# A graph network kernel: edge scores, segment softmax and weighted sums as one stage with an online softmax, on one core

## The chip, the core and the metric

The kernel runs on one core of a Trainium2 chip. The metric is the device time of one execution in microseconds (us); the time before is the median of three runs. Matmuls run on TensorE (PE), elementwise work on VectorE (DVE) and ScalarE (ACT), gathers are issued by GpSimd (POOL), the other transfers by SyncE (SP) and ScalarE. SBUF is the on-chip memory, PSUM takes what TensorE computes.

## What is computed

A graph of 12,500 nodes with 256 features and 200,000 edges, sorted by destination, goes through two blocks. The first is graph attention with 8 heads of 32 columns, the second two graph convolutions and a dense layer. The first block is what the change rewrites:

```python
h = (relu(layernorm(x)) @ W.T).reshape(n, H, D)
h_src, h_dst = h[src], h[dst]
alpha = einsum('ehd,hd->eh', h_src, a_src) + einsum('ehd,hd->eh', h_dst, a_dst)
enc = relu(edge_attr @ edge_W.T + edge_b).reshape(-1, H, D)
alpha = alpha + sum(enc * h_dst, axis=-1)
alpha = where(alpha >= 0, alpha, 0.2 * alpha)
amax = segment_max(alpha, dst, n)
ex = exp(alpha - amax[dst])
attn = ex / maximum(segment_sum(ex, dst, n)[dst], 1e-10)
out = segment_sum(h_src * attn[..., None], dst, n).reshape(n, H * D) + bias
```

## The kernel before

Nodes lie in 98 tiles of 128. The program is a row of stages (functions ending in `_phase`), each closed by a barrier of all engines. Edges are cut into chunks of 128; a chunk that straddles two node tiles is worked through once for each, which makes 1664 steps, 16 steps to an iteration, 104 iterations.

`steps_phase` loads the edges, finds the tile and the rows of each step, and writes the lists to HBM. `node_phase` (through `dense_phase`) normalizes each tile of nodes and multiplies it by W; the result stays in SBUF (`h_all`) for the destination side and goes to HBM (`gat_table`) for the source side. `score_phase` computes a score for each edge and head. For a pair of chunks TensorE encodes the edge attributes (L870, bf16, in three parts that together hold a float32) and spreads the destination rows to the edges by a one-hot matmul in float32 (L875). ScalarE applies the relu (L772), VectorE multiplies (L817), sums over the 32 columns of each head (L820), and makes the one-hots (L807). GpSimd gathers the source rows, 128 at a time (L757), for their source scores; the gathered rows are stored to HBM (`gathered`). `softmax_phase` loads all scores, turns them so that a head's edges run along a row, scans for each segment's maximum forwards and backwards, takes the exponential and stores the weights. `gat_sum_phase` reads the gathered rows and weights back, multiplies on GpSimd (L1145), and TensorE adds the rows of a chunk to their nodes by a one-hot matmul (L1187), whose result VectorE adds to the accumulator `acc` (L1166); ScalarE makes those one-hots (L1093, L1100). `mid_phase` divides by the weights' sum, adds the bias and the residual and makes the first convolution's table.

`units_phase` lists the edges a second time for the convolutions, in pairs of chunks (units, 256 edges). `conv_phase`, run twice, gathers rows of a table into a ring of `NB` = 4 blocks of `PB` = 8 pairs (L1513), and TensorE sums them to nodes (L1607). What sets the order everywhere is the code as written: each engine has one queue, and the engines meet at semaphores (`wait_ge`).

Of the kernel before, what the change touches and what calls it, by code (L numbers as in the profile page):

```python
# [26 lines left out]
P = 128  # L27
# [3 lines left out]
CHUNKS = -(-EDGES // P)  # L31
TILES = -(-NODES // P)
LAST = NODES - (TILES - 1) * P
Q = -(-(CHUNKS + TILES - 1) // P)
STEPS = Q * P
LANES = 16
ITERS = STEPS // LANES
PL = P // LANES
PARTS = 3
AROW = PARTS * 3 * P  # L40
EROW = 3 * P + AROW // 2
ENC = PARTS * PARTS * 3 + PARTS
HROW = HEADS + FEAT + 1
HCOL = HROW + HEADS
DROW = HCOL - HEADS
H0, H1 = HEADS, HEADS + FEAT
GT = 7
# [4 lines left out]
EPP = Q * P  # L52
FULL_P = EDGES // EPP
REST = EDGES - FULL_P * EPP
# [3 lines left out]
UL = 8  # L58
UITERS = -(-(PAIRS + TILES - 1) // UL)
# [4 lines left out]
PB = 8  # L64
NB = 4
BLOCKS = -(-PAIRS // PB)

# [34 lines left out]
def gnn(nc, A, out):  # L102
# [19 lines left out]

    edge_rows = dram("edge_rows", (STEPS, EROW))
    chunk_end = dram("chunk_end", (STEPS,))
    tile_of = dram("tile_of", (STEPS,), I32)
    dloc_rows = dram("dloc_rows", (ITERS, LANES, P), BF16)
    attr_rows = dram("attr_rows", (ITERS, LANES, AROW), BF16)
    enc_parts = dram("enc_parts", (PARTS, 4, FEAT), BF16)
    start_rows = dram("start_rows", (STEPS, P))
    gat_table = dram("gat_table", (TILES * P, HROW))  # L130
    gathered = dram("gathered", (ITERS, P, LANES * HROW))
    score_rows = dram("score_rows", (ITERS, P, LANES * HEADS))
    weight_rows = dram("weight_rows", (ITERS, P, LANES * HEADS))
# [4 lines left out]
    pair_rows = dram("pair_rows", (UNITS, PAIR))  # L138
    unit_end = dram("unit_end", (UNITS,))
    unit_slot = dram("unit_slot", (UNITS,), I32)  # L140
    unit_need = dram("unit_need", (UNITS,), I32)
    unit_tile = dram("unit_tile", (UNITS,), I32)
    src_blocks = dram("src_blocks", (UNITS // PB, P, 2 * PB), I32)

# [6 lines left out]
    with top:  # L151
        src_col = sb(top, "src_col", [P, STEPS], I32)
        dloc_col = sb(top, "dloc_col", [P, STEPS])
        tiles_row = sb(top, "tiles_row", [1, STEPS], I32)
# [3 lines left out]
        const = (src_col, dloc_col, tiles_row, iota_row, part_id, ident)  # L158

        steps_phase(nc, sb, ps, sem, A, const, edge_rows, chunk_end, tile_of, dloc_rows, attr_rows,  # L160
                    start_rows)
        end_phase()
        with ExitStack() as ctx:
            h_all = sb(ctx, "h_all", [P, TILES, HCOL])
            node_phase(nc, sb, ps, sem, pair, held, A, const, h_all, gat_table)
            end_phase()
            score_phase(nc, sb, ps, sem, pair, held, A, const, h_all, gat_table, gathered, dloc_rows,
                        attr_rows, enc_parts, score_rows)
            end_phase()
        softmax_phase(nc, sb, ps, sem, pair, held, const, start_rows, score_rows, weight_rows)  # L170
        end_phase()
        with ExitStack() as ctx:
            acc1 = sb(ctx, "acc1", [P, TILES, F1])
            dinv = sb(ctx, "dinv", [P, TILES])
            x1_norm = [sb(ctx, f"x1_{n}", [P, TILES]) for n in ("scale", "shift")]
            with ExitStack() as ctx2:
                acc = sb(ctx2, "acc", [P, TILES, HROW])
                gat_sum_phase(nc, sb, ps, sem, pair, held, const, acc, acc1[:, 0:2 * LANES, :], gathered, weight_rows)
# [3 lines left out]
            dlu_col = sb(ctx, "dlu_col", [P, 2 * UNITS])  # L182
# [26 lines left out]
def steps_phase(nc, sb, ps, sem, A, const, edge_rows, chunk_end, tile_of, dloc_rows, attr_rows,  # L209
# [3 lines left out]
    with ExitStack() as ctx:  # L213
# [32 lines left out]
        def part(n):  # L246
            return parts[:, :, n * 3 * P:(n + 1) * 3 * P].rearrange("p q (f e) -> p q f e", e=P)
# [1703 lines left out]
```

## Time and profile before

| what | value |
|---|---|
| time, median of 3 runs | 8444.61 us (8442.0 to 8444.65) |
| the profiled execution | 8437.87 us |
| its span in the profile | 8436.0 us |
| TensorE, VectorE busy | 56%, 49% |
| ScalarE, GpSimd busy | 20%, 66% |
| mean granted TensorE clock | 0.687 of full |

The busy shares are averages over stages with different limits; a table by stage says more. The granted clock has two levels, 1.2 GHz (0.50) and 2.4 GHz (1.00); a number between them is a stretch that had both.

### The profile page before, as it was taken

To read this page: it belongs to the slowest core of one execution; us is meant where nothing else is said; L and a number is where in the kernel's file an instruction comes from. 1 tells how busy PE (TensorE), PEld (TensorE's weight loads), DVE (VectorE), ACT (ScalarE), POOL (GpSimd) and SP (SyncE) were. 2 spreads that over 40 slices of the span, in tenths; PEclk is the share of its full clock that TensorE was granted. 3 is DMA by queue.
4 is the path that set the end of the run, shared out by engine and by line. 5 is a ranking of instruction groups with operands and counts; after the bars stand their busy time and mean duration, and the time that the engine had idled before them with its cause. 6 is when DMAs were issued, how large, how long until landed. Compare 5 with 4: busy or idle time off the path is not lost. (4 is left out here: it accounts for less than half of the span.)

```text
span 8436.0 us, 106625 instructions
## 1 busy us (share of the span) xinstructions
PE 4713.9 (56%) x18446; PEld 3436.2 (41%) x18447; DVE 4133.2 (49%) x11501; ACT 1707.6 (20%) x4219; POOL 5566.8 (66%) x5281
## 2 busy tenths in 40 slices
PE   0677777777760588884233333333455555555547
PEld 0544343343430456553233333333344454444534
DVE  3577777777754788887222222222343232232225
ACT  1422222222211688873000000000010000000001
POOL 1177777777750488874477777777637777777771
PEclk8877777777775799997656666566655555555555
DMA  4587878787872577764222222222111111111115
GB/s 111 165 259 251 252 250 252 251 252 250 253 220 24 170 247 246 245 227 138 68 52 52 52 52 52 52 52 52 44 31 41 40 41 41 40 41 41 41 28 186
DMA packets 565146, 1089.10 MB, mean 129 GB/s; under 512 B 232605, under 2 KB 387847, under 8 KB 511476
## 3 DMA queue, kind: packets, MB, share of 16 engines
q1 hardware_dynamic: 316250, 635.91, 22.6%
q0 software_dynamic: 181344, 387.13, 18.2%
q10 hardware_dynamic: 67506, 65.57, 2.9%
q8 instruction: 14, 0.23, 0.0%
q14 instruction: 32, 0.26, 0.0%
HBM read 774.01 MB, written 314.19 MB: 129 GB/s over the span
## 5 line engine op out<-in xcount | busy, mean ns | idle before, releaser
L1513 POOL DMA_INDIRECT c_g<-conv_table,c_idx x3128 | 3004.1, 960 | 1039.1 <-issue 911.2
L1607 PE MATMUL c_sums<-c_g,c_S 128*128 x7040 | 1489.2, 400 | 2178.1 <-POOLq L1503 1732.4
L1607 PEld LDWEIGHTS c_sums<-c_g,c_S 128*128 128x128 f32 x7040 | 1404.5, 305 | 2278.0 <-issue 2277.6
L757 POOL DMA_INDIRECT sc_g<-gat_table,sc_idx x1664 | 1580.4, 950 | 506.8 <-issue 506.5
L1579 DVE TENSOR_TENSOR acc<-acc,c_sums 128x128 f32 (+1 forms) x1760 | 444.9, 253 | 2446.5 <-PE c_sums L1607 2394.7
L875 PE MATMUL sc_dstp<-h_all,sc_onehot 128*128 x3328 | 1281.2, 520 | 412.8 <-DVE sc_dsts L818 410.7
L875 PEld LDWEIGHTS sc_dstp<-h_all,sc_onehot 128*128 128x128 f32 x3328 | 732.9, 244 | 757.4 <-issue 649.6
L1187 PE MATMUL gs_sums<-gs_g,acc 128*128 128x265 f32 x3328 | 808.4, 400 | 157.4 <-DVE acc L1166 135.7
L1145 POOL TENSOR_TENSOR gs_g<-gs_g,gs_wt 128x1024 f32<-128x1024 f32 x416 | 783.7, 1909 | 153.9 <-DMA gs_wt<-weight_rows 152.0
L1166 DVE TENSOR_TENSOR acc<-acc,gs_sums 128x132 f32 (+1 forms) x3328 | 781.3, 293 | 164.7 <-PE gs_sums L1187 153.0
L772 ACT ACTIVATE sc_enc<-sc_encp 128x512 f32<-128x512 f32 x832 | 496.9, 597 | 1582.3 <-PE sc_encp L870 1083.2
L1187 PEld LDWEIGHTS gs_sums<-gs_g,acc 128*128 128x128 f32 x3328 | 567.0, 190 | 398.8 <-DVE acc L1166 319.9
L817 DVE TENSOR_TENSOR sc_prod<-sc_enc,sc_dstp 128x512 f32<-128x512 f32 x832 | 566.4, 681 | 178.6 <-PE sc_dstp L875 170.4
L1570 DVE TENSOR_TENSOR c_S<-iota_row,c_dcol 128x512 f32<-128x512 f32 x880 | 555.1, 692 | 40.9 <-DVE c_dcol L1566 39.9
L820 DVE TENSOR_REDUCE sc_dots<-sc_prod 128x16 f32<-128x512 f32 x832 | 570.8, 686 | 0.0
L1093 ACT ACTIVATE acc<-iota_row,gs_dcol 128x128 f32<-128x128 f32 x1664 | 530.8, 389 | 137.2 <-PE gs_sums L1187 125.8
L1694 ACT ACTIVATE n_square<-acc 128x2048 f32<-128x2048 f32 (+3 forms) x14 | 18.3, 1322 | 2301.3 <-DVE acc L1668 2300.9
L870 PE MATMUL sc_encp<-sc_ew,sc_att 30*128 30x256 bf16 x1664 | 378.9, 314 | 121.8 <-issue 121.7
L1297 ACT ACTIVATE fc_rows<-fc_x,x_shift,x_scale 128x256 f32<-128x256 f32 x98 | 58.8, 600 | 1690.1 <-issue 1649.2
L807 DVE TENSOR_SCALAR sc_onehot<-sc_dl,part_id 128x256 f32<-128x256 bf16 x832 | 309.8, 373 | 45.9 <-DVE sc_score L843 39.6
L870 PEld LDWEIGHTS sc_encp<-sc_ew,sc_att 30*128 30x128 bf16 x1664 | 94.5, 96 | 511.1 <-issue 373.1
L1100 ACT ACTIVATE acc<-acc,iota_row 128x512 f32<-128x512 f32 x416 | 284.3, 707 | 0.4
(221 smaller groups left out, 3422.1 us busy)
## 6 DMA issues: line engine op xcount, KB each, us to landing
gathered<-sc_g SPq DMA_DIRECT2D x208, 1060.0 KB
gs_g<-gathered SPq DMA_DIRECT2D x208, 1060.0 KB
sc_dl<-dloc_rows SPq DMA_DIRECT2D x104, 512.0 KB
c_g<-conv_table,c_idx POOLq DMA_INDIRECT x3128
sc_g<-gat_table,sc_idx POOLq DMA_INDIRECT x1664
gat_table<-h_all ACTq DMA_DIRECT2D x14, 927.5 KB
x_rows<-md_x SPq DMA_DIRECT2D x14, 896.0 KB
fc_x<-x_rows ACTq DMA_DIRECT2D x98, 128.0 KB
```

Source lines behind the costliest of these rows:

```text
L757: pool.indirect_dma_start(G[u][:, b, :], None, gat_table, bass.IndirectOffsetOnAxis(idx[v][:, b:b + 1], 0)).then_inc(rows_in[u][k], 16)
L772: nc.scalar.activation(enc[r][:, :, :], enc_p[r][:, :, :], ACT.Relu).then_inc(relu_done, 1)
L817: nc.vector.tensor_tensor(prod[r][:, :, :], enc[r][:, :, :], dst_p[r][:, :, 0:FEAT], ALU.mult).then_inc(prod_done, 1)
L820: nc.vector.reduce_sum(dots[:, 2 * q * HEADS:2 * (q + 1) * HEADS], prod[r][:, :, :].rearrange("p s (h d) -> p (s h) d", d=HDIM), AXX).then ...
L875: last = nc.tensor.matmul(dst_p[r][:, s, 0:DROW], onehot[q % DEPTH][:, s * P:(s + 1) * P], flat[:, bass.ds(tiles[2 * q + s] * HCOL + HEADS ...
L1093: last = nc.scalar.activation(S[:, u * LANES + c, :], iota_row[:, :], ACT.Abs, scale=-1.0, bias=dcol[u][:, c:c + 1])
L1145: nc.gpsimd.tensor_tensor(h, h, spread(w, [[HEADS, QUART], [1, HEADS], [0, HDIM]]), ALU.mult).then_inc(mul_done, 1)
L1166: nc.vector.tensor_tensor(t, t, sums[:, b % R, c], ALU.add).then_inc(add_done, 1)
L1187: nc.tensor.matmul(sums[:, b % R, 0:HROW], S[:, u * LANES + b, :], G[u][:, b, :], start=True, stop=True).then_inc(sum_done, 1)
L1513: pool.indirect_dma_start(G[:, v * PC + j, :], None, table, bass.IndirectOffsetOnAxis(idx[v][:, j:j + 1], 0)).then_inc(rows_in[v], 16)
L1570: nc.vector.tensor_tensor(S[:, u * CH + 2 * b:u * CH + 2 * b + 4, :], spread(iota_row[:, :], [[0, 4], [1, P]]), spread(dcol[u][:, 2 * b:2 ...
L1607: last = nc.tensor.matmul(sums[:, b % R, 0:width], S[:, u * CH + 2 * b + j, :], flat[:, bass.ds(slots[b] * (2 * width) + j * width, width) ...
```

## The change

`steps_phase`, `score_phase`, `softmax_phase` and `gat_sum_phase` go. One `units_phase` lists the edges once, as units of 256, with their flags of segment starts, for all later stages. `node_phase` no longer keeps `h_all`: it writes the source table (now with each head's 32 columns led by a one, 272 columns) and, new, the node rows as three bf16 parts (`h_parts`), which GpSimd splits. `gat_phase` does scores, softmax and sums in one loop over 110 iterations of 8 units. In a slot of the loop the scores of iteration t (8 quanta, each one half of the columns of two units) are interleaved with the softmax and the sums of iteration t − 1. The gathered rows stay in an SBUF ring of 4 blocks of 4 pairs until they are weighted. The softmax is online: the maximum of a segment is that within the iteration, and what was summed before is rescaled when it grows (`rescale`). The sum over a head's 32 columns moves from VectorE to TensorE (`dot`, against a 0/1 matrix `mask` of 4 columns), the addition of the source scores too (`source`), and the weighting moves from GpSimd to VectorE (`weigh`). The convolutions load their tables from HBM at their start and have blocks of 4 pairs (`PB`) instead of 8.

```diff
@@ constants
-PB = 8
+PB = 4
 NB = 4
@@ node_phase, GpSimd, once for each of 14 groups of 7 tiles
+                nc.gpsimd.tensor_tensor(rest[:, :, :].rearrange("p t (h d) -> p t h d", d=HDIM), h,
+                                        at[0].rearrange("p t (h d) -> p t h d", d=HDIM), ALU.subtract).then_inc(split, 1)
...
+                nc.gpsimd.tensor_copy(at[1], rest[:, :, :]).then_inc(split, 1)
...
+                nc.gpsimd.tensor_tensor(at[2], rest[:, :, :], at[1], ALU.subtract).then_inc(parts_done, 1)
@@ gat_phase, VectorE
+                def transposed(t, u, i, d):
...
+                    dve.wait_ge(dst_done, 2 * n + 2)
+                    nc.vector.tensor_scalar(oht[d % 2][:, :], dl[u][:, d * W2:(d + 1) * W2], part_id[:, 0:1], None, ALU.is_equal).then_inc(oht_done, 1)
+                def product(n, r):
+                    dve.wait_ge(relu_done, n + 3)
+                    dve.wait_ge(dst_done, n + 5)
+                    dve.wait_ge(dots_done, n + 1)
+                    nc.vector.scalar_tensor_tensor(prod[r], enc[r], a_dst[:, r:r + 1], dst_p[r][:, :], ALU.add, ALU.mult).then_inc(prod_done, 1)
...
+                def weigh(m, b, slot):
+                    n = UL * m + b
+                    dve.wait_ge(back_done, m + 2)
+                    dve.wait_ge(sum_done, n + 3)
...
+                def flush(m, b, tile):
...
+                    nc.vector.tensor_tensor(at, at, sums[b % 2][:, 0:WROW], ALU.add).then_inc(add_done, 1)
@@ gat_phase, TensorE
+                def quantum(t, u, i, q):
+                    n, r, d, c = QS * t + q, q % 2, q // 2, q % 2
...
+                    pe.wait_ge(relu_done, n + 2)
+                    nc.tensor.matmul(enc_p[:, :], ew[:, c * P:(c + 1) * P], att[u][:, d * W2:(d + 1) * W2], start=True, stop=True).then_inc(enc_done, 1)
+                    if c == 0:
+                        pe.wait_ge(h_in[d], 32 * (t + 1))
+                        pe.wait_ge(oht_done, DS * t + d + 1)
+                    pe.wait_ge(prod_done, n + 1)
+                    for b in range(2):
+                        for k in range(PARTS):
+                            last = nc.tensor.matmul(dst_p[r][:, b * PAIR:(b + 1) * PAIR], hr[:, 2 * d + b, k, c * P:(c + 1) * P],
+                                                    oht[d % 2][:, b * PAIR:(b + 1) * PAIR], start=k == 0, stop=k == PARTS - 1)
+                    last.then_inc(dst_done, 1)
+                def dot(t, u, q):
...
+                    pe.wait_ge(prod_done, n + 3)
...
+                    for j in range(4):
...
+                        last = nc.tensor.matmul(to, prod[r][:, j * P:(j + 1) * P], mask[:, :], start=q == 0 and j == 0, stop=True, skip_group_check=True)
+                    last.then_inc(dots_done, 1)
...
+                def add(m, b):
+                    n = UL * m + b
+                    pe.wait_ge(wg_done, n + 1 + USED)
+                    pe.wait_ge(onehot_done, n + 1)
+                    pe.wait_ge(add_done, n + 1)
+                    for j in range(2):
+                        last = nc.tensor.matmul(sums[b % 2][:, 0:WROW], S[b % 4][:, j, :], wg[b % 2][:, j, :], start=j == 0, stop=j == 1)
+                    last.then_inc(sum_done, 1)
@@ conv_phase
+                load_ends(nc, sp, free_f, unit_end, s_ends)
+                sp.dma_start(table_row[0:1, :, :], AP(unit_table.tensor, 0, [[0, 1], [UNITS, 3], [1, UNITS]])).then_inc(s_lists, 16)
```

Three places of the order matter. On TensorE, in the score loop before, a pair of chunks takes these rows (`sc_encp` is the encoding, `sc_dstp` the destination rows; ISA and REGISTER_ALU are register work):

```order
L870 MATMUL sc_encp<-sc_ew,sc_att 128x256 x2
L875 ISA
L875 MATMUL sc_dstp<-h_all,sc_onehot 128x265
L875 ISA
L875 MATMUL sc_dstp<-h_all,sc_onehot 128x265
```

In the middle of a slot of the changed kernel TensorE has these (`ga_back` the exponentials turned back, `ga_dots` the sums over a head, `ga_sums` the weighted rows; `acc` here is scratch):

```order
L1299 MATMUL ga_back<-ident,ga_ex 128x128
L1249 MATMUL ga_dots<-ga_mask,acc 128x4 x4
L1229 REGISTER_ALU
L1230 MATMUL ga_encp<-ga_att,ga_ew 128x512
L1233 REGISTER_ALU
L1237 MATMUL ga_dstp<-ga_oht,ga_h 128x256 x6
L1303 REGISTER_ALU
L1304 REGISTER_ALU
L1307 MATMUL ga_sums<-ga_wg,acc 128x265 x2
L1303 REGISTER_ALU
L1304 REGISTER_ALU
L1307 MATMUL ga_sums<-ga_wg,acc 128x265 x2
```

Between encodings of twice the size TensorE now has four dots that move 4 columns each, six matmuls for the destination rows in place of one for each chunk, and the sums' matmuls, which were a stage of their own.

On VectorE, one quantum of the score loop before reads thus (product, copy, sum over a head, one-hot):

```order
L817 TENSOR_TENSOR sc_prod<-sc_enc,sc_dstp 128x512
L818 COPY sc_dsts<-sc_dstp 128x18
L820 TENSOR_REDUCE sc_dots<-sc_prod 128x16
L807 TENSOR_SCALAR sc_onehot<-sc_dl,part_id 128x256
L814 REGISTER_ALU
L816 REGISTER_ALU
```

In the first half of a slot of the changed kernel, from quantum 2's product to the one-hot of quanta 4 and 5 (`ga_t` holds the segment maxima, `ga_oht` the one-hot):

```order
L1087 SCALAR_TENSOR_TENSOR acc<-acc,ga_a_dst,ga_dstp 128x512
L1125 ISA
L1128 SCALAR_TENSOR_TENSOR ga_t<-ga_flags,ga_soft,ga_f 128x128
L1129 SCALAR_TENSOR_TENSOR ga_t<-ga_flags,ga_soft,ga_g 128x128
L1109 REGISTER_ALU
L1130 TENSOR_TENSOR ga_t<-ga_t 128x128
L1109 REGISTER_ALU
L1131 TENSOR_TENSOR ga_t<-ga_soft,ga_t 128x128
L1085 REGISTER_ALU
L1087 SCALAR_TENSOR_TENSOR acc<-acc,ga_a_dst,ga_dstp 128x512
L1080 ISA
L1081 TENSOR_SCALAR ga_oht<-ga_dl,part_id 128x512
```

The reduction is gone; the one-hot that TensorE's quantum 4 waits for now stands behind two products and the four instructions on the maxima, which themselves wait for TensorE's carries.

## Rows read from the trace of the kernel before

**Rows 1.** Busy time by stage (engine busy and count, PEclk, DMA share, GB/s)

```profile
...
0.00:187.00 187.00, 6.60 (x26) 4.71 (x27) 70.24 (x50) 27.69 (x31) 22.06 (x27) 0.87 0.44 117
...
187.00:378.00 191.00, 126.81 (x600) 96.34 (x600) 88.95 (x363) 92.99 (x312) 0.92 (x1) 0.87 0.53 147
...
378.00:2478.00 2100.00, 1561.35 (x4992) 827.50 (x4992) 1503.80 (x3853) 506.29 (x933) 1583.14 (x1667) 0.76 0.80 250
...
2478.00:2830.00 352.00, 44.86 (x214) 32.96 (x214) 167.28 (x93) 54.42 (x43) 0.00 (x0) 0.53 0.30 55
...
2830.00:3796.00 966.00, 808.41 (x3328) 567.04 (x3328) 792.34 (x3330) 805.10 (x2393) 794.59 (x417) 0.99 0.74 242
...
4030.00:4098.00 68.00, 7.07 (x28) 5.09 (x28) 19.03 (x32) 6.88 (x28) 9.89 (x10) 0.53 0.32 72
...
4098.00:6094.00 1996.00, 731.82 (x3520) 684.56 (x3520) 545.73 (x1432) 0.00 (x0) 1503.73 (x1564) 0.61 0.20 52
...
```

**Rows 2.** The page's groups of the gathers

```profile
...
L757 POOL DMA_INDIRECT sc_g<-gat_table,sc_idx x1664 | 1580.4, 950 | 506.8 <-issue 506.5
...
L1513 POOL DMA_INDIRECT c_g<-conv_table,c_idx x3128 | 3004.1, 960 | 1039.1 <-issue 911.2
...
```

**Rows 3.** Score stage in order of time: start, length, engine, wait before

```profile
...
1004.44 0.29 DVE L840 TENSOR_TENSOR sc_dots<-sc_dots,sc_g 128x128 f32<-128x128 f32 x1 [3.09 <-DMA sc_g<-gat_table,sc_idx]
...
1006.71 2.13 PE L875 MATMUL sc_dstp<-h_all,sc_onehot 128*128 x4 [4.91 <-DVE sc_dsts L818]
...
```

**Rows 4.** Groups by line of the score and sum stages: busy, mean ns, idle before

```profile
...
L870 PE MATMUL sc_encp<-sc_ew,sc_att 30*128 30x256 bf16 x1664 | 378.9, 314 | 121.8 <-issue 121.7
...
L1187 PE MATMUL gs_sums<-gs_g,acc 128*128 128x265 f32 x3328 | 808.4, 400 | 157.4 <-DVE acc L1166 135.7 <-POOL gs_g L1145 21.7
...
L817 DVE TENSOR_TENSOR sc_prod<-sc_enc,sc_dstp 128x512 f32<-128x512 f32 x832 | 566.4, 681 | 178.6 <-PE sc_dstp L875 170.4 <-issue 6.2
...
L1166 DVE TENSOR_TENSOR acc<-acc,gs_sums 128x132 f32 (+1 forms) x3328 | 781.3, 293 | 164.7 <-PE gs_sums L1187 153.0 <-DVE acc L1166 0.3
...
L1145 POOL TENSOR_TENSOR gs_g<-gs_g,gs_wt 128x1024 f32<-128x1024 f32 x416 | 783.7, 1909 | 153.9 <-DMA gs_wt<-weight_rows 152.0
...
L1150 DVE MEMSET acc<- 128x12985 f32 x1 | 10.9, 10879 | 10.7 <-issue 10.7
...
```

**Rows 5.** TensorE in order of time at full clock, scores and first convolution

```profile
...
1000.31 1.16 PE L875 MATMUL sc_dstp<-h_all,sc_onehot 128*128 x4
...
1001.41 0.39 PE L870 MATMUL sc_encp<-sc_ew,sc_att 30*128 30x256 bf16 x2
...
4999.82 1.75 PE L1607 MATMUL c_sums<-c_g,c_S 128*128 x12 [2.33 <-DVE c_S L1570]
...
```

**Rows 6.** TensorE in order of time: weight loads at half clock, and a wait

```profile
...
224.55 1.78 PEld L630 LDWEIGHTS wp<-heads,w_sb 128*128 128x128 f32 x8 [2.89 <-issue]
...
6201.25 3.11 PEld L1789 LDWEIGHTS pj_op<-w,pj_yT 128*128 128x128 f32 x14
...
1017.53 0.38 PE L870 MATMUL sc_encp<-sc_ew,sc_att 30*128 30x256 bf16 x2 [0.60 <-issue]
...
```

**Rows 7.** Granted clock in short stretches of the mid stage and the project stage

```profile
...
3922.60:3926.00 3.40, 2.43 (x17) 1.68 (x15) 1.48 (x3) 3.40 (x9) 0.00 (x0) 1.00 0.59 208
...
3926.00:3929.40 3.40, 0.93 (x6) 0.69 (x6) 3.37 (x8) 1.27 (x4) 0.00 (x0) 1.00 0.76 234
...
3929.40:3932.80 3.40, 3.27 (x12) 2.50 (x12) 2.52 (x16) 0.91 (x4) 0.00 (x0) 0.50 0.51 170
...
6200.00:6250.00 50.00, 50.00 (x242) 50.00 (x241) 20.39 (x35) 9.50 (x10) 0.00 (x0) 0.50 0.20 50
...
```

**Rows 8.** VectorE in order of time, without and with GpSimd arithmetic beside it

```profile
...
298.09 0.17 DVE L466 TENSOR_SCALAR nd_var<-nd_mv 128x7 f32<-128x7 f32 x1
...
3879.25 2.52 DVE L466 TENSOR_SCALAR md_var<-md_mv 128x7 f32<-128x7 f32 x1
...
3882.37 3.20 DVE L470 SCALAR_TENSOR_TENSOR md_shift<-md_mv,md_rstd 128x7 f32<-128x7 f32 x1
...
```

More of the change, by code:

```diff
@@ L611, in dve_before @@
+            for c in range(2):
+                for q in range(4):
+                    last = nc.vector.tensor_copy(heads[q * HDIM:(q + 1) * HDIM, c, c * 4 + q:c * 4 + q + 1],
+                                                 score[q * HDIM:(q + 1) * HDIM, c:c + 1])
             last.then_inc(s_heads, 1)
@@ new lines, in iteration @@
+                def iteration(a, u, i, more):
+                    scores(a, u)
+                    sp.wait_ge(stab_in[u], 16 * (i + 1))
+                    take_waits(sp, held)
+                    tiles = registers(stab[u][0:1, :], mybir.EngineType.SP, 0, TILES - 1)
+                    if more:
+                        tiles_of(a + 1, 1 - u)
+                    nodes(a, 0, tiles)
+                    nodes(a, 1, tiles)
+                    if not isinstance(a, int) or a >= 1:
+                        units(a - 1, 1 - u)
+                    nodes(a, 2, tiles)
+                    nodes(a, 3, tiles)
@@ new lines, in source @@
+                def source(m, u, i):
+                    pe.wait_ge(list_in[u], 96 * (i + 1))
+                    take_waits(pe, held)
+                    slot_of = registers(utab[u][0:1, 1, :], mybir.EngineType.PE, 0, NS - 1)
+                    need = registers(utab[u][0:1, 2, :], mybir.EngineType.PE, READY + 1, READY + 1 + UNITS // PB)
+                    for b in range(UL):
+                        pe.wait_ge(rows_ready, need[b])
+                        rows = G[:, bass.ds(slot_of[b] * PROWS, PROWS)].rearrange("p (j c) -> p j c", c=HROW)[:, :, S0:HROW]
+                        last = nc.tensor.matmul(dots.rearrange("p (h s) -> p s h", s=CH)[:, 2 * b:2 * b + 2, :], ident[:, :], rows,
+                                                start=False, stop=True, skip_group_check=True)
+                    last.then_inc(score_done, 1)
@@ new lines, in carries, with factors @@
+                def carries(m, u):
+                    pe.wait_ge(kept_done, m + 2)
+                    one = ones[0:1, 0:1]
+                    nc.tensor.matmul(carry[:, 0:1], line[u][0:1, 0:P], one, start=True, stop=True)
+                    nc.tensor.matmul(carry[:, 1:2], line[u][0:1, P:2 * P], one, start=True, stop=True).then_inc(carry_done, 1)
+                def factors(m):
+                    pe.wait_ge(ef_done, m + 2)
+                    pe.wait_ge(diff_done, m + 2)
+                    nc.tensor.matmul(fac_p, ones[:, :], ef[:, :], start=True, stop=False)
+                    nc.tensor.matmul(fac_p, ones[:, :], less[:, :], start=False, stop=True).then_inc(facp_done, 1)
@@ L1455, in conv_phase, with load_frees @@
+def load_frees(nc, row):
+    _, regs = nc.values_load_multi_w_load_instructions(
+        row, engines=[mybir.EngineType.Pool], min_val=USED, max_val=USED + UNITS,
+        skip_runtime_bounds_check_because="unit numbers are clamped where they are worked out")
+    return regs
+def conv_phase(nc, sb, ps, sem, pair, held, const, lists, name, width, acc, table, fc=None):
+    iota_row = const[0]
+    unit_end, unit_table, src_blocks, dlu_blocks = lists[0:4]
     R = 4
-    CH = 2 * UL
-    PC = 2 * PB
```

1599 lines of the change are left out of this document (803 added, 796 removed).

## The prediction

> **What bounds the kernel now.** I read the stages first [rows 1]. Six of them are what the change rewrites: the steps stage (0 to 187 us), the node stage (191 us), the score stage (2100), the softmax stage (352), the sum stage (966) and the units stage (68). Together they take 3864 us. Everything else takes 8436 − 3864 = 4572 us, the two convolutions most of it. The reader is to see that the score stage and the convolutions have one bound. The score stage issues 1664 gathers, each with 950 ns of work and about 0.30 us of gap [rows 2], so one every 1.25 us, and 1664 × 1.25 = 2080 of the stage's 2100 us. VectorE waits 3.09 us for a gather at the end of an iteration, and TensorE 4.91 us behind it [rows 3]: TensorE is busy 74% of this stage and is not its bound. The sum stage is the opposite: GpSimd no longer gathers, TensorE is busy 808 of 966 us at a clock of 0.99, and all engines but SyncE are close to full. The softmax stage is a chain of single instructions and transfers.
>
> **What the change does to GpSimd.** The scores and sums share one gather of each row. It has 1564 gathers instead of 1664, 1955 us at 1.25 us each. The whole softmax stage goes, and so do the stores of the gathered rows and their reading back. If the new stage were still bound by its gathers, it would replace 2100 + 352 + 966 = 3418 us by 1955 and save about 1460 us. The question is what an iteration of 8 units (16 chunks of 128 edges), a slot, costs the other engines. There are 110 of them, 111 with the ends of the pipeline; the gathers of one take 1955/110 = 17.8 us.
>
> **TensorE in one slot, at full clock.** A float32 matmul is two records in the trace. I count records by the order.
> Adding up the weighted rows: 8 units × 2 chunks × 2 = 32 records of 265 columns. The sum stage has 808.4 us for 3328 of them, 0.243 us each [rows 4]; four in the score stage take 1.10 us, from 1000.31 to 1001.41 [rows 5]. At 0.25 that is 8.0 us.
> The dot products over the 32 columns of a head leave VectorE (its reduction is gone) and become 32 float32 matmuls that move only 4 columns each behind a fresh load of 128 columns: 64 records. The nearest rows are loads at half clock: eight with 16 columns moved take 1.78 us, fourteen with 64 columns moved 3.11 us, so 0.22 each [rows 6]; and at full clock twelve records with 128 columns take 1.75 us, 0.146 each with the last one's tail [rows 5]. From below, half of 0.22 is 0.11. I take 0.12, nearer to the rows with few columns: 7.7 us, with 7.0 and 9.3 as bounds.
> The source scores, 8 such matmuls with 16 columns: 16 × 0.12 = 1.9 us.
> The rows of the destination nodes, 48 bf16 matmuls of 256 columns. The bf16 records of the score stage have 378.9/1664 = 0.228 us at mixed clock [rows 4], and two of them at full clock 0.39 us with tail [rows 5]. A float32 record passes 265 columns in 0.25, and bf16 needs one pass of the two, so about 0.13: 6.2 us (bounds 5.2 and 7.4). The 8 encodings of 512 columns, twice that: 2.1 us.
> Turning the scores and exponentials, lines, carries and factors: 24 records, 2.9 us. Loading 16 registers: 0.6 us, the issue gap of the score stage's iteration [rows 6].
> The sum is 8.0 + 7.7 + 1.9 + 6.2 + 2.1 + 2.9 + 0.6 = 29.4 us. TensorE alone is thus well above the 17.8 us of the gathers.
>
> **The Trainium skill on the small matmuls.** The rows put a float32 weight load of 128 columns at 0.22 us at half clock [rows 6]. The Trainium skill (TensorE: Matmul & The Clock Gate, section LDWEIGHTS) gives columns divided by 1.2, so 107 ns, with no word on float32; this trace disagrees with it by a factor of two. By the page's figure the 80 small records would be an estimate of half as dear, some 4.8 us less in a slot, and the total about 530 us lower. The sum above goes by the rows.
>
> **The other engines in one slot.** VectorE: 8 products of 512 columns at 0.68 [rows 4], overlapped 0.60; 8 weightings of 528 columns, about 0.62; 8 additions of 265 columns, twice the 132 columns' 0.235 (781.3/3328) less their second start, 0.38; 4 one-hots; 4 scans; a dozen small ones; 16 registers. That is 4.8 + 5.0 + 3.0 + 2 + 1.6 + 2.6 + 1.2, about 20 us. ScalarE keeps its relus and one-hots, (506 + 805)/110 = 12 us. Both are under TensorE.
>
> **The waits between them.** The order rows show where TensorE and VectorE wait for one another. The quanta 4 and 6 and the next slot's quantum 0 need a one-hot which VectorE makes only after a product and after steps of the softmax chain (tops, weigh 0 and 1). I walked through the slot with the prices above: TensorE waits about 1.1, 1.3 and 0.9 us there, and 1.1 us at the slot's start, where the last addition and VectorE's register loads stand ahead of product 0. With 29.4 that makes 33.8 us: the slot if the clock stays full. Queued behind each of these waits on TensorE are the dots, and behind them VectorE's next product.
>
> **The clock.** It does not stay full by itself. In the mid stage the stretch with TensorE busy 0.93 of 3.40 us is followed by one at half clock, the stretch with 2.43 busy by a full one [rows 7]. The project stage is busy 50.00 of 50 us and never leaves 0.50: its work is loads of 128 columns with 64 moved [rows 7]. That is the work of the dots. In the first half of a slot TensorE has four dots and four quanta, a few tiny matmuls and most of the waits, so that it moves few columns, as in the stretch ahead of that fall; I expect the clock to fall there in most slots. In the second half the additions move columns as densely as the sum stage, which ran at 0.99, and bring it back. From the middle of the first half until the second pair of additions about 7.5 us of full-clock work runs at half clock, 7.5 us more, of which the waits of above absorb half: 33.8 + 3.7 = 37.5 us.
>
> **The sum.** The new stage: zeroing 25,970 columns, twice the 10.9 us of [rows 4], with the loads and the constants before it, 45 us; 110 × 37.5 = 4125; 10 for the ends: 4180 us.
> The node stage: three GpSimd instructions a group of 1792 columns to split the table. The 1024-column one takes 1.91 us, so these 3.3 each, 10 us a group, as long as a group is now (about 136/14 = 9.7). While GpSimd works, two small VectorE instructions of a group last 2.52 and 3.20 us instead of 0.17 [rows 8]: 5.4 × 14 = 75 us more, 265 us (bounds 191 and 340).
> Edges listed once: 187 + 68 become one stage with 7 gathers and whole-table stores, but some 30 us of VectorE flags behind them: 170 us (160 to 220).
> The convolutions: 1996 us for 1564 × 1.25 = 1955, so all boundaries and ends cost 41 us. Half-size blocks double the boundaries, and the list is now loaded at their start: 30 us each, 60 in all (bounds 0 and 100). What is queued behind a POOL wait for a block is the next gather, and this engine is the bound there.
> 4572 + 60 + 170 + 265 + 4180 = 9247 us of span. The profiled execution is 1.9 us over its span, the median 6.7 us over the profiled one, so 9255 for the median; I say 9250.
>
> **The rivals.** (1) The clock holds: slot 31 to 35 us, 33.8 likeliest, 5067 + 55 + 110 × 33.8 = 8840 us. For it: the sum stage's 0.99, and waits that are all short. Against it: the stretches of [rows 7]. Chance 0.24.
> (2) Faster: the dots' loads hide, one mechanism. If the 80 small records cost 0.06 us because they slide under their neighbours' columns, a slot is 33.8 − 4.8 = 29, and the waits are partly used: 28 to 29. The point that decides is (8436 − 5122)/110 = 30.1 us a slot. It would give about 8250 us. Against it is that such records stand next to one another, each load as long as in [rows 6]. Chance 0.12.
> (3) The clock is mostly at half, because the additions come in pairs of 2 us between dots and do not lift it in time: slot 43 to 60 us, 9900 to 11,700 us. For it: the project stage, busy throughout at 0.50. Chance 0.15.
> (4) The change does not do what it says, its gathers bound the stage again at 18 us a slot: 7100 us; it needs TensorE at 18 where 29 are counted, chance 0.02.
> My forecast, bound by TensorE with a clock that falls and rises (slot 35 to 43 us, 8970 to 9850 us), has 0.47.
>
> **How the numbers follow.** Predicted 9250. The range 8500 to 10,200 holds the forecast (0.47), all of (1) (0.24) and the near third of (3) with the bounds of the node stage, some 0.8; the forecast's own range is 8970 to 9850. A measurement tells some 0.2% from no change. Faster: (2) and (4) without the part that ends just at the point, 0.13; same 0.02; slower 0.85.
>
> **What the profile after would show.** TensorE busy over 85% of the new stage with VectorE near 55% and GpSimd under 50%; VectorE's products waiting for the destination rows; the granted clock between 0.7 and 0.9 there with falls inside each slot; 64 dot records at about 0.12 us at full clock; a node stage near 265 us, no slower a gather. I am wrong if the small records cost much less than 0.11, if the clock sits at either of its two levels throughout, or if a wait that I priced at 1 us (the one-hots behind the softmax chain) is several.

## The result and the profile after

The changed kernel takes 9882.8 us (median of four runs, 9862.0 to 9903.5) against 8443.3 us (8415.8 to 8444.7): a ratio of 1.171, 95% interval 1.168 to 1.175. It is slower by 1440 us. That lies in the stated range (8500 to 10,200 us), 633 us above the predicted time and just outside the forecast's own range (8970 to 9850 us). The profiled execution has a span of 9860.3 us. Its stages, in the columns of [rows 1] (node, the new stage, mid, first convolution, project):

```profile
180.00:380.00 200.00, 130.86 (x600) 98.63 (x600) 100.52 (x353) 117.58 (x407) 121.97 (x42) 0.95 0.69 230
380.00:5301.00 4921.00, 4427.69 (x21122) 3447.74 (x21122) 2089.45 (x4754) 1645.61 (x4015) 1482.34 (x1566) 0.67 0.33 96
5301.00:5541.00 240.00, 117.19 (x588) 96.80 (x588) 171.12 (x385) 84.41 (x212) 102.78 (x28) 0.71 0.42 135
5541.00:7537.50 1996.50, 834.61 (x3520) 757.83 (x3520) 548.15 (x1431) 0.00 (x0) 1512.23 (x1564) 0.56 0.21 52
7644.00:7684.00 40.00, 31.75 (x283) 31.38 (x282) 24.06 (x42) 10.66 (x12) 0.00 (x0) 0.88 0.41 95
```

One new stage of 4921 us stands where 2100 + 352 + 966 = 3418 us stood [rows 1]. TensorE is busy 90% of it, VectorE 42%, GpSimd 30%, and the granted clock is 0.67. The costliest groups of the page that belong to the stage:

```profile
L936 POOL DMA_INDIRECT acc<-gat_table,ga_idx x1564 | 1481.8, 947 | 3377.3 <-DVE ga_wg L1147 2593.0
...
L1249 PE MATMUL ga_dots<-ga_mask,acc 128*128 128x4 f32 x7040 | 1286.5, 306 | 244.5 <-DVE acc L1087 244.5
...
L1237 PE MATMUL ga_dstp<-ga_oht,ga_h 128*128 128x256 bf16 x5280 | 1103.5, 370 | 191.4 <-DVE ga_oht L1081 185.4
L1307 PE MATMUL ga_sums<-ga_wg,acc 128*128 128x265 f32 x3520 | 1227.7, 509 | 2.4 <-DVE ga_wg L1147 1.1
...
L1147 DVE TENSOR_TENSOR ga_wg<-acc,ga_back 128x528 f32<-128x528 f32 x880 | 610.2, 704 | 1155.9 <-PE ga_sums L1307 886.9
L1157 DVE TENSOR_TENSOR acc<-acc,ga_sums 128x265 f32 x880 | 375.1, 426 | 529.4 <-PE ga_sums L1307 529.4
```

GpSimd, the bound of the score stage before [rows 2], now stands idle 3377 us ahead of its gathers, most of it until VectorE has weighed rows and so freed a buffer. A gather itself is as long as before (947 ns). VectorE waits for the sums of TensorE. Everything hangs on TensorE, and TensorE spends most of this stage at its lower clock. One slot of it in order of time (start, length, line, wait before in brackets):

```profile
2632.37 1.05 PE L1249 MATMUL ga_dots<-ga_mask,acc 128*128 128x4 f32 x8 [2.12 <-DVE acc L1087]
...
2635.59 1.87 PE L1249 MATMUL ga_dots<-ga_mask,acc 128*128 128x4 f32 x8
...
2651.46 1.46 PE L1237 MATMUL ga_dstp<-ga_oht,ga_h 128*128 128x256 bf16 x6 [0.41 <-DVE ga_oht L1081]
2652.72 3.31 PE L1307 MATMUL ga_sums<-ga_wg,acc 128*128 128x265 f32 x8
2655.86 0.95 PE L1249 MATMUL ga_dots<-ga_mask,acc 128*128 128x4 f32 x8
...
2662.06 1.27 PE L1237 MATMUL ga_dstp<-ga_oht,ga_h 128*128 128x256 bf16 x6 [1.27 <-DVE ga_oht L1081]
...
2674.90 1.05 PE L1249 MATMUL ga_dots<-ga_mask,acc 128*128 128x4 f32 x8 [2.50 <-DVE acc L1087]
```

The same slot as stretches of time (length, TensorE busy with its records, granted clock, DMA share, GB/s):

```profile
2628.00:2635.00 7.00, 4.70 (x31) 1.00 0.57 161
2635.30:2655.30 20.00, 19.58 (x82) 0.50 0.18 52
2655.40:2662.20 6.80, 5.53 (x37) 1.00 0.48 136
2662.60:2665.50 2.90, 2.90 (x10) 0.50 0.84 251
2665.60:2675.60 10.00, 7.50 (x54) 0.99 0.50 147
```

The reader is to see three things. Eight dot records that take 0.95 us at full clock take 1.87 at half. After the slot's first wait the clock falls to its lower level and stays there for 20 us, although TensorE is busy 19.58 of them. It comes back at the end of the first pair of additions (3.31 us, 1.96 at full clock); a wait of 1.27 us later in the slot is followed by another fall, this one short. From the first dot (437.8 us) to the last (5273.9) a slot takes 44.0 us on average. The slot shown is one of the milder ones: it has 23 us at the lower level, the mean slot 29, and in the next slot the clock falls three times (at about 2676, 2706 and 2713 us) and comes back within a pair of additions each time.

### The profile page after: what moved, and what is told of

Read it like the earlier page. It is cut to its first block and busy times, and to the rows that moved or that the text cites. A ratio compares the mean times of both kernels' runs of the same rounds, so it can differ in the third digit from the quotient of the medians.

```text
span 9860.3 us, 131430 instructions
## 1 busy us (share of the span) xinstructions
PE 6824.7 (69%) x31008; PEld 5513.5 (56%) x31009; DVE 3750.0 (38%) x8947; ACT 2007.6 (20%) x4935; POOL 4783.6 (49%) x4792
## 5 line engine op out<-in xcount | busy, mean ns | idle before, releaser
L936 POOL DMA_INDIRECT acc<-gat_table,ga_idx x1564 | 1481.8, 947 | 3377.3 <-DVE ga_wg L1147 2593.0
L1249 PEld LDWEIGHTS ga_dots<-ga_mask,acc 128*128 128x128 f32 x7040 | 1304.5, 272 | 303.7 <-DVE acc L1087 259.6
L1249 PE MATMUL ga_dots<-ga_mask,acc 128*128 128x4 f32 x7040 | 1286.5, 306 | 244.5 <-DVE acc L1087 244.5
L1237 PE MATMUL ga_dstp<-ga_oht,ga_h 128*128 128x256 bf16 x5280 | 1103.5, 370 | 191.4 <-DVE ga_oht L1081 185.4
L1307 PE MATMUL ga_sums<-ga_wg,acc 128*128 128x265 f32 x3520 | 1227.7, 509 | 2.4 <-DVE ga_wg L1147 1.1
L1147 DVE TENSOR_TENSOR ga_wg<-acc,ga_back 128x528 f32<-128x528 f32 x880 | 610.2, 704 | 1155.9 <-PE ga_sums L1307 886.9
L1307 PEld LDWEIGHTS ga_sums<-ga_wg,acc 128*128 128x128 f32 x3520 | 882.6, 263 | 204.4 <-DVE ga_wg L1147 3.4
L1237 PEld LDWEIGHTS ga_dstp<-ga_oht,ga_h 128*128 128x128 bf16 x5280 | 578.5, 124 | 686.8 <-DVE ga_oht L1081 187.1
L1087 DVE SCALAR_TENSOR_TENSOR acc<-acc,ga_a_dst,ga_dstp 128x512 f32<-128x512 f32 x880 | 651.7, 741 | 188.6 <-issue 166.1
L983 ACT ACTIVATE acc<-iota_row,ga_dcol 128x128 f32<-128x128 f32 x1760 | 600.7, 391 | 336.6 <-PE ga_sums L1307 336.6
```

The lines of the kernel that those rows point to most:

```text
L936: pool.indirect_dma_start(G[:, (v * PC + j) * HROW:(v * PC + j + 1) * HROW], None, gat_table, bass.IndirectOffsetOnAxis(idx[:, c:c + 1], 0 ...
L983: last = nc.scalar.activation(S[b % 4][:, j, :], iota_row[:, :], ACT.Abs, scale=-1.0, bias=dcol[u][:, 2 * b + j:2 * b + j + 1])
L1087: nc.vector.scalar_tensor_tensor(prod[r], enc[r], a_dst[:, r:r + 1], dst_p[r][:, :], ALU.add, ALU.mult).then_inc(prod_done, 1)
L1147: nc.vector.tensor_tensor(wg[b % 2][:, :, 0:S0].rearrange("p j (h d) -> p j h d", d=HCOLS), rows, spread(back[:, 2 * b:P], [[1, 2], [CH, H ...
L1237: last = nc.tensor.matmul(dst_p[r][:, b * PAIR:(b + 1) * PAIR], hr[:, 2 * d + b, k, c * P:(c + 1) * P], oht[d % 2][:, b * PAIR:(b + 1) * P ...
L1249: last = nc.tensor.matmul(to, prod[r][:, j * P:(j + 1) * P], mask[:, :], start=q == 0 and j == 0, stop=True, skip_group_check=True)
```

## Experiments

A slot below is the time from the first dot to the last over 110 (where a kernel has none, from the encodings), "stage clock" the granted clock between them, "idle" the time in it in which TensorE is not busy, also over 110. The table puts the measured times together; the kernel before had 8438 to 8444 us beside them.

| run | time, us (runs) | ratio to before, 95% | slot, us | stage clock | TensorE idle in a slot, us |
|---|---|---|---|---|---|
| after | 9883 (4) | 1.168 to 1.175 | 44.0 | 0.67 | 4.0 |
| e1_guard | 9889 (4) | 1.171 to 1.177 | 44.0 | 0.67 | 3.9 |
| e2_order | 9022 (4) | 1.065 to 1.073 | 36.5 | 0.73 | 0.2 |
| e3_wide | 8935 (2) | 1.051 to 1.069 | 34.8 | 0.97 | 5.6 |
| e4_fill | 9430 (2) | 1.115 to 1.123 | 39.5 | 0.77 | 1.2 |
| e5_best | 8192 (5) | 0.969 to 0.974 | 28.6 | 0.99 | 0.3 |
| e6_best64 | 8273 (4) | 0.978 to 0.984 | 29.3 | 0.95 | 0.3 |
| e7_nodots | 9099 (2) | 1.076 to 1.083 | 36.9 | 0.72 | 9.3 |
| e8_nodots_order | 8118 (2) | 0.959 to 0.964 | 28.1 | 0.81 | 2.9 |
| e9_first | 8203 (4) | 0.969 to 0.973 | 28.6 | 0.97 | 0.3 |
| e10_last | 8667 (2) | 1.024 to 1.029 | 33.0 | 0.82 | 0.2 |

Two theories stood against each other; 0.50 and 1.00 of the granted clock are its two levels, 1.2 and 2.4 GHz. A, the mix: the clock falls and stays down because much of TensorE's work moves few columns. B, the waits: it falls because TensorE stands still twice a slot.

**e1_guard, the control.** All experiments but this differ from it and not from the changed kernel itself.

```diff
-                    pool.wait_ge(wg_done, free)
+                    pool.wait_ge(wg_done, smax(free, 1))
...
-                        pe.wait_ge(rows_ready, need[b])
+                        pe.wait_ge(rows_ready, smax(need[b], 1))
```

> The control for all that follow: the changed kernel with one register operation more ahead of each wait that is against a number read from a table (8 a slot or iteration on TensorE, one a block on GpSimd), a maximum with 1, which changes no value. Both theories expect the same: TensorE +0.4 us a slot (8 at 0.05) where nothing hides it, 44 us, and GpSimd 391 blocks at 0.05 us, 20 us, in each convolution: 9900 to 9970 us against 9883.

Measured 6 us more than the changed kernel, within what runs differ by, and below the expectation: slot and convolutions are as long as before, so the register operations cost nothing that shows. The experiments can be read against either.

**e2_order: the waits taken away.**

```diff
-                    if a:
-                        product(n, 0)
                     if bc:
                         scans(m, v, im)
                     if a:
                         product(n + 1, 1)
-                        transposed(t, u, i, 1)
+                        transposed(t, u, i, 2)
...
                         weigh(m, 7, slot_of[7])
-                        for b in range(5, UL):
+                    if more:
+                        product(n + 8, 0)
+                    if bc:
+                        for b in range(5, UL):
```

> The control with VectorE's order changed: each one-hot for the destination rows is made one place earlier (as soon as its buffer is free), and the product that the next slot's first dots wait for stands ahead of the last three additions. This takes away TensorE's waits, 2.1 to 2.5 us at a slot's start, 1.3 and 0.4 us later, about 4.1 us in 44.3. Theory A (the mix): the clock falls since dots move 4 columns behind loads of 128, and only the additions lift it; the waits go but the first half still runs at half clock: slot 40 us, about 9460 us. Theory B (the waits): the clock falls because TensorE stands still, and stays down by no other cause; without waits it holds: slot 28 to 30 us (27.1 us of records at full clock by the trace of after), 8150 to 8350 us.

Measured 867 us under the control. Two of TensorE's stretches, from the first additions to the next slot's quantum 2 and from there to the additions (the columns are those of the last stretches above):

```profile
2628.60:2643.80 15.20, 14.90 (x100) 1.00 0.58 169
2645.60:2664.30 18.70, 18.70 (x73) 0.50 0.19 57
```

The whole stage, in the columns of [rows 1]:

```profile
440.00:4451.00 4011.00, 3990.41 (x21015) 3177.38 (x21015) 2042.81 (x4690) 1634.28 (x3984) 1451.60 (x1532) 0.73 0.40 116
```

TensorE is now busy 3990 of 4011 us and still spends half its time at the lower clock: the stretch of 18.70 us is busy without a break. So B is not the whole cause. But A's number (40 us) was too high as well: 44.0 − 36.5 = 7.5 us went, and only 3.8 us of them were waits. The rest came through the clock: in the two slots looked at it holds from the end of the first additions to the slot's last additions or a quantum into the next slot, without a fall in between.

**e3_wide: the same loads, more columns behind them.**

```diff
-                        to = dots.rearrange("p (h s) -> p h s", s=CH)[:, c * (HEADS // 2):(c + 1) * (HEADS // 2), 4 * d + j]
-                        last = nc.tensor.matmul(to, prod[r][:, j * P:(j + 1) * P], mask[:, :], start=q == 0 and j == 0, stop=True, skip_group_check=True)
+                        to = dots_p[:, P:2 * P]
+                        last = nc.tensor.matmul(to, prod[r][:, j * P:(j + 1) * P], ident[:, :], start=q == 0 and j == 0, stop=True, skip_group_check=True)
```

> The control with each dot matmul moving 128 columns instead of 4, behind the same loads, into a part of the bank that nobody reads; the scores thus lack the dot products (only the source scores are left). Records of 128 columns have 0.146 us at full clock against 0.12, so it is 1.7 us more work a slot. Theory A (the mix, few columns moved): the clock holds or falls for much less time, slot 33 to 38 us, 8700 to 9200 us, faster than the control although it does more. Theory B (the waits): the clock falls after the same waits and the slot takes 45 to 46 us, 9950 to 10,100 us.

The kernel leaves out the sums over a head. Measured 953 us under the control with more work in it and all waits still there. The stage, in the columns of [rows 1]:

```profile
440.00:4263.00 3823.00, 3206.63 (x21020) 2546.57 (x21019) 2030.03 (x4693) 1633.74 (x3984) 1451.87 (x1532) 0.97 0.42 122
```

TensorE is busy 84%, less than in e2_order, at a clock of 0.97. This is the run that tells A from B: waits of 0.9 to 2.5 us are all still in the slot (5.6 us, more than the control's 3.9), and what was changed is the columns moved. The clock does fall in some slots (to 0.50 from about 2692.6 to 2699.2 us, for one), but its mean is 0.97. Eight dot records have 1.05 to 1.16 us here at full clock, against 0.95 to 1.05.

**e4_fill: the waits filled instead of removed.** The operand `pad` holds zeros.

```diff
+                def extra(count):
+                    for _ in range(count):
+                        nc.tensor.matmul(dots_p[:, P:4 * P], pad[:, 0:P], pad[:, :], start=False, stop=True, skip_group_check=True)
...
                     if bc:
                         turn(m, v)
+                        extra(12)
...
                         dot(t, u, 6)
+                        extra(6)
```

> The control with TensorE's two longest waits filled: 12 bf16 matmuls of 384 columns of zeros (1.9 us at full clock) after the turn at a slot's start and 6 of them ahead of quantum 0 of the next slot. Nothing reads their result. Theory B (the waits): TensorE never stands still, the clock holds, slot 31 to 33 us, 8500 to 8700 us. Theory A (the mix): the clock falls later in the first half and comes back with the additions as before; slot 41 to 46 us, 9550 to 10,100 us.

Measured 459 us under the control: below A's range, far above B's. In the slots looked at the clock held some 1 to 3 us longer, fell all the same, and came back in the first additions. Idle time went from 3.9 to 1.2 us a slot, with about 3.2 us of filler in its place (2.12 and 1.14 us for the two groups), so that the 4.5 us won in a slot came through the clock.

**e5_best and e6_best64: both edits, with the right result.** The mask is widened so that each dot adds zeros to the columns that aren't its own.

```diff
-        mask = sb(ctx, "ga_mask", [P, HEADS // 2])
+        mask = sb(ctx, "ga_mask", [P, HEADS // 2 * CH + CH - 1 + P])
...
+                        at = (HEADS // 2 * CH + CH - 1) - (c * (HEADS // 2) * CH + 4 * d + j)
+                        last = nc.tensor.matmul(dots, prod[r][:, j * P:(j + 1) * P], mask[:, at:at + P], start=q == 0 and j == 0, stop=True, skip_group_check=True)
```

> VectorE's new order (as e2_order) together with dots that move 128 columns, now with the right result: each dot multiplies by a slice of a wider mask, 128 columns of which only the 4 of its heads hold ones, and adds into all 128 columns of the scores. Theory A (few columns moved let the clock fall): without waits and with the clock up, the slot is the work at full clock, 26.7 us (36.8 us at 0.73 in e2_order) + 0.8 (8 x 1.05 against 8 x 0.95 us for the eight records of a quantum) = 27.5 to 29; stage 3100 to 3250, total 8030 to 8200 us, 3 to 5% under the kernel before. Theory B (the waits alone) has fallen for the largest part by e2_order; its rest says that what e3_wide won came with its long waits in which the chip rests, and without these the clock falls again: slot 35 to 37 us, 8850 to 9050 us.

> As e5_best with 64 columns moved by each dot instead of 128. If a record of 64 columns costs 0.12 us and is wide enough to hold the clock, the slot is 27 us, 8000 to 8150 us, equal to or just under e5_best. If the clock follows the columns moved, it lies between e2_order (4 columns, 9022) and e5_best: the clock 0.8 to 0.95 in the stage, slot 29 to 33 us, 8200 to 8700 us. Theory B's rest: as e2_order, 9000 us.

e5_best takes 8192 us: 1691 under the changed kernel and 2.9% under the kernel before. Its stage:

```profile
440.00:3582.00 3142.00, 3111.62 (x21022) 2508.71 (x21021) 2031.74 (x4692) 1634.42 (x3984) 1452.31 (x1532) 0.99 0.51 149
```

Its first dot of a slot in order of time, with no wait ahead of it:

```profile
2642.26 1.16 PE L1255 MATMUL ga_dots<-ga_mask,acc 128*128 128x128 f32 x8
```

TensorE is busy 99% at a clock of 0.99 and hardly a wait is left, so that this slot, 28.6 us, is TensorE's work at full clock; without the 0.8 us that 128 columns cost over 4, it is 27.8 us of the changed kernel's own work. Half as many columns (e6_best64) give 0.95 and 81 us more, the second of its expectations:

```profile
440.00:3661.00 3221.00, 3190.28 (x21038) 2592.97 (x21037) 2038.16 (x4694) 1634.54 (x3984) 1452.49 (x1532) 0.95 0.50 145
```

e2_order, e6_best64 and e5_best differ in nothing but the columns of the dots (4, 64, 128) and the mask behind them; TensorE is busy 99% in all three, and the stage's clock is 0.73, 0.95 and 0.99. B's rest, that e3_wide's clock held thanks to its long waits, expected 8850 to 9050 us and is out.

**e7_nodots and e8_nodots_order: the dots left out.** The first matmul of the source scores now starts the sum in their place.

```diff
-                    for j in range(4):
...
-                        last = nc.tensor.matmul(to, prod[r][:, j * P:(j + 1) * P], mask[:, :], start=q == 0 and j == 0, stop=True, skip_group_check=True)
-                    last.then_inc(dots_done, 1)
+                    pe.sem_inc(dots_done, 1)
```

> The control without the 32 dot matmuls of a slot (the scores lack the dot products, only the source scores are left); everything else, waits and VectorE's order too, as in after. Theory A: 7.6 us of narrow work a slot go and with them what holds the clock down: 19.5 us of records at full clock and waits that VectorE (18.7 us busy) and GpSimd (17.8) set, slot 23 to 27 us, 7550 to 8000 us. Were the dots worth only their own records at the clock of after (0.183 x 64 = 11.7 us), the slot would be 32.6 us at a clock still near 0.67, 8600 us.

> e7_nodots with VectorE's order of e2_order (the scores lack the dot products). e7_nodots took 37.0 us a slot at a clock of 0.72 although TensorE's narrow work was gone: its waits had grown to about 10 us. Theory A in its new form (what counts is how many columns TensorE moves in a stretch: narrow dots lower it, and standing still just as much): the order takes the waits away until VectorE or GpSimd bind (18.7 us busy and some 3 us of registers and hand-overs, or 17.8): slot 23 to 28 us, clock 0.85 or more, 7550 to 8150 us. If the softmax chain between TensorE, VectorE and ScalarE is what binds a slot without dots, it stays at 30 us or more, 8300 us and up, with TensorE waiting on it.

e7 came out above both expectations: 9099 us, 500 over the cautious one. The chain of waits shows why (time waited in total, count, longest, over 3600 us):

```profile
PE ga_dstp L1238 <- DVE ga_oht L1082: 653.0, 387, 2.3
...
PE ga_encp L1231 <- DVE acc L1088: 250.2, 108, 2.8
```

What had been dots became waits for one-hots and products, 9.3 us a slot, and the clock was at 0.72 with not one narrow dot in it. So A had to be widened: the narrow dots are not the only thing beside which the clock is low here; in e7 long waits stand in their place. e8, with the waits reduced to 2.9 us, gives 8118 us, at the upper end of what A expected; its slot (28.1 us) is just over the 28 and its clock (0.81) under the 0.85. The other branch, a softmax chain that binds the slot at 30 us or more, is out. Against e5_best it also prices the wide dots: some 8.4 to 9 us of TensorE records a slot are in e5_best and not in e8, and the slot is 0.5 us longer (74 us in the whole kernel). The wide dots stand where e8 has waits and a lower clock; how much of their price each of the two pays was not separated.

**e9_first and e10_last: where in the slot the columns count.**

```diff
+                        if q < 4:
+                            to, by = dots, mask[:, at:at + P]
+                        else:
+                            at = HEADS // 2 * CH + CH - 1
+                            to = dots.rearrange("p (h s) -> p h s", s=CH)[:, c * (HEADS // 2):(c + 1) * (HEADS // 2), 4 * d + j]
+                            by = mask[:, at:at + HEADS // 2 * CH:CH]
```

(e10_last has `q >= 4`.)

> e5_best with the 128-column dots only in the slot's first half (quanta 0 to 3); the four dots that have additions next to them move 4 columns again. Theory A: where additions stand next to the dots the clock held with narrow dots too (e2_order: 1.00 from 2628.5 to 2643.9), so only the first half needs the columns: clock 0.97, slot 0.4 us shorter (4 x 0.1), 8140 to 8180 us. If the columns of the whole slot count, the clock lies between e2_order (0.73) and e5_best (0.98) and the time between 8300 and 8700 us.

> The mirror of e9_first: 128 columns in the dots of quanta 4 to 7, 4 columns in those of the first half. Theory A: the clock falls in the first half as in e2_order and comes back with the additions; slot 36 to 37 us, 8950 to 9050 us. If the columns of the whole slot count, it comes out like e9_first.

e9 has the slot of e5_best (28.6 us, clock 0.97) with wide dots in only half of it; its time, 8203 us, is equal to e5's within the runs, not under it as A expected (its profiled execution also had a node stage 20 us longer). e10 has the same number of columns moved in a slot and takes 464 us more. One stretch on either side of its fall:

```profile
2636.00:2655.00 19.00, 18.67 (x128) 1.00 0.63 186
2657.00:2669.00 12.00, 12.00 (x52) 0.50 0.20 55
```

So in this kernel it isn't the sum over the slot that decides but where the wide dots stand: they win most in the first half, where no additions stand next to the dots. e10 is also 354 us under e2_order, which A did not expect. In the two slots looked at the clock falls later (at about 2629 and 2656 us, 8 and 4.5 us after the slot's first dot; in e2_order 3 us after it or ahead of it) and comes back a quantum earlier, behind the first wide dots and some 0.4 us ahead of the first additions. So the additions are not the only work beside which it rises. In the first of the two slots the stretch in which it rises (at about 2635.8 us) and the first additions behind it:

```profile
2635.36:2637.07 1.71, 1.71 (x10) 0.86 0.39 122
...
2636.19 1.96 PE L1319 MATMUL ga_sums<-ga_wg,acc 128*128 128x265 f32 x8
```

## Why the prediction was right, and where its sizes were wrong

The mechanism of the prediction held: GpSimd is no longer the bound, TensorE is, its work alone is above the 17.8 us of the gathers, and the clock falls and rises within each slot and adds to it. The sizes, against the prediction's own terms (in us; slot terms times 110):

| term | predicted | measured | difference in the total |
|---|---|---|---|
| TensorE's work in a slot at full clock | 29.4 | 27.8 | −176 |
| its waits in a slot | 4.4 | 4.0 | −44 |
| the clock, in a slot | 3.7 | 12.2 | +935 |
| zeroing, constants, ends | 55 | 81 | +26 |
| node stage | 265 | 200 | −65 |
| units stage | 170 | 180 | +10 |
| both convolutions, over before | 60 | 12 | −48 |
| project stage | 66 | 40 | −26 |
| mid, norms, final | as before | +1 | +1 |
| **sum** | **9247** | **9860** | **+613** |

(27.8 is from e5_best, which has another order on VectorE; the waits are the stage's idle time over 110; the clock is what is left, 44.0 − 27.8 − 4.0.)

That the total stayed in the stated range is in part luck. The clock alone was 935 us too low; with it and without the terms that came out under their prices (359 us together) the span would be 10,219 us, above the range's 10,200. And the range reached beyond 9850 us only for a share of rival 3 and for the bounds of the node stage.

**The clock was the most mis-sized term.** The prediction said that it falls in the slot's first half and that the additions of the second bring it back. Both are in the stretches above. It sized the fall at 7.5 us of full-clock work, from the middle of the first half, and let waits absorb half of it. In the trace it begins right after the first quantum, lasts 20 us to the end of the first additions, and comes a second time after the wait of 1.27 us; at a mean of 0.67, two thirds of the 44.0 us, 29 us, are at the lower level. Waits absorb less than was said: e3_wide, at 0.97 and in the same order, idles 5.6 us a slot and the changed kernel 4.0, so some 1.6 us and not 3.8. The slot is thus outside the forecast's own 35 to 43 us, at the lower edge of rival 3 (43 to 60 us, "mostly at half"). That rival had the size but not the reason: it said that pairs of additions do not lift the clock in time, and in the two slots looked at each fall ends within a pair. The forecast had the reason but not the size.

**The rows that spoke for it were read too mildly.** The prediction cited the project stage, busy 50.00 of 50 us at 0.50 [rows 7], for the fall and for rival 3, and still sized the fall by the short stretch alone. e2_order's 18.70 us of unbroken work at 0.50 is the same picture, and e5_best, the same order with wide dots, is at 0.99.

**The work.** Dots: 0.119 us a record at full clock (0.95 for eight) against 0.12, right, and rival 2, which needed 0.06, is out. Additions: 1.96 us for eight records with the tail, the next work 1.79 later, 0.224 each against 0.25. Encoding and destination rows: a quantum takes 0.98 us (2656.75 to 2657.73) against 1.04. These small excesses add up to the 1.6 us and a little more.

**The Trainium skill on the loads.** At full clock the dots' records follow each other every 0.111 us, at half clock every 0.225 (eight in 1.80 us). The Trainium skill (TensorE: Matmul & The Clock Gate, section LDWEIGHTS) gives the columns divided by 1.2, 107 ns for 128, and names no clock. The trace agrees at full clock and not at half. The prediction set the figure beside a half-clock row, called it a factor of two apart and put the page's case 530 us lower. But its sum went by 0.12 us and not by 0.22: by the page's figure the 80 records are, as an estimate, 1.0 us a slot and some 115 us in the total under it.

**The waits** of the slot shown are 0.18 + 0.41 + 1.27 + 2.50 = 4.4 us, the mean slot's idle time 4.0. The prediction's walk through the slot was for full clock, and e3_wide, which has the order of the changed kernel and a clock of 0.97, nearly bears it out: 0.94 and 1.33 us at quanta 4 and 6 and 1.10 at the next slot's quantum 0, against 1.1, 1.3 and 0.9. At half clock the first two shrink to nothing and 0.41. What was mis-sized is the slot's start, 2.1 to 2.5 us against 1.1. "VectorE's products waiting for the destination rows" was wrong: they waited 21.5 us for them in all, and VectorE's long waits are for the sums (887 and 529 us). That e2_order won 7.5 us a slot by taking away 3.8 us of waits says that here a wait also cost clock; the prediction counted the two apart.

**The node stage.** GpSimd's three instructions take 3.45 + 1.68 + 3.58 = 8.7 us a group against 10. The small VectorE instructions beside them:

```profile
L491 DVE SCALAR_TENSOR_TENSOR nd_shift<-nd_mv,nd_rstd 128x7 f32<-128x7 f32 x14 | 11.9, 853 | 0.5
...
L487 DVE TENSOR_SCALAR nd_var<-nd_mv 128x7 f32<-128x7 f32 x14 | 5.2, 370 | 1.0
```

On the mean they are held for 0.20 and 0.69 us above the 0.17 us that both have in the node stage before, not for 2.35 and 3.03 as in the mid stage [rows 8]: 12 us in all instead of 75. The price was taken from one instance of each and multiplied by 14. Only one of the fourteen groups here came near it (3.14 us).

**The convolutions.** Halved blocks and the list at the start cost 0 and 12 us; a gather has 967 ns and the engine's gaps are as before. Why the boundaries of the smaller blocks cost nothing was not tried.

What the prediction wanted to see: TensorE over 85% (90%), GpSimd under 50% (30%), falls inside the slots, dot records at 0.12 us and gathers no slower are there; the clock (0.67) is under its 0.7, VectorE (42%) under its 55% because the stage is longer (18.6 us a slot against 20), and the node stage is not.

## What to carry to other kernels

Before matmuls with a handful of columns behind full weight loads take over work from another engine, price them at the lower clock too, and with them everything that stands next to them: here that was the largest error of the sum. Where TensorE is the bound and its granted clock is low although it is busy, let the thin matmuls move more columns (zeros in a wider mask, added into the whole tile, cost 0.1 us for eight records here) in the thinnest stretch, and order the other engines so that what TensorE needs next is made one step early: the two edits together took a kernel that was 17% slower to one that is 2.9% faster. Read the clock by stretches of a few us inside an iteration, since a stage's mean hides which part is thin.

## What the runs showed of the hardware

**Busy is not enough for the clock.** e2_order was busy 18.70 of 18.70 us at 0.50 until additions came; e3_wide, idle 16% of its stage, ran at 0.97. The Trainium skill (TensorE: Matmul & The Clock Gate, section Why this matters for your kernels) says to keep TensorE busy continuously for the full clock. The trace disagrees with this as all that is needed: e2_order, e6_best64 and e5_best are all busy 99% of the stage and have 0.73, 0.95 and 0.99, and they differ in the columns of their dots.

**The same work can hold either level.** The project stage has the same 196 matmuls of 64 columns in every kernel. Before, it ran at 0.50 [rows 7], and so it did in e3_wide to e9_first. In the changed kernel the clock rose within two us of the first of them (7644.4 us) and was 1.00 from 7646 us to the last; e1_guard, e2_order and e10_last are alike. The row of its matmuls after (shortest, median and longest in ns, first and last start):

```profile
L1891 PE MATMUL pj_op<-w,pj_yT x196: 222/275/470, 7644.4 to 7675.5; 128*128 128x64 f32 x196
```

The same in e5_best:

```profile
L1897 PE MATMUL pj_op<-w,pj_yT x196: 314/421/469, 5948.9 to 6007.1; 128*128 128x64 f32 x196
```

Of the twelve kernels four rose to the upper level in the work's first 2.5 us and kept it; eight were at the lower one to its end, TensorE busy throughout. Why it rose in those four and not in the others was not tried. It is worth 26 us here. In the new stage's slot the like would explain why the fall lasts until the additions, but that is not shown.
